# Graph network on one core: 28 products of zeros per unit between an edge layer's product and its transpose

## The chip, the core and the metric

The kernel runs on one core of a Trainium2 chip. The engines are TensorE (PE, with its weight loads shown as PEld), VectorE (DVE), ScalarE (ACT), GpSimd (POOL) and SyncE (SP, which only issues transfers here). The metric is the device time of one execution in microseconds, the median over runs.

## The reference

A residual chain of four graph blocks over 3125 nodes with 128 features and 100000 edges, sorted by destination. The third block matters here. It runs the same edge layer three times:

```python
h = x @ W_enc + b_enc
ea = edge_attr @ W_ee + b_ee            # 16 attributes of an edge -> 128 features
for i in range(3):
    m = relu(h[src] + ea) * edge_atten  # one message of 128 features per edge
    aggr = segment_sum(m, dst)          # summed over the edges of each destination
    z = (1.0 + eps[i]) * h + aggr
    ...                                 # two small matrix products per node, then the next h
```

The other blocks are a two-layer attention convolution, a mean aggregation and a graph attention; the change does not touch them.

## The kernel before

The stages run one after another. In the trace, the two attention convolutions take about the first 3.1 ms (their edge stages are `conv_edges`, with L716, L724 and L768 on TensorE), and the three edge layers of the third block (`gine_edges`, called at L1832) follow, each with a node stage (`gine_nodes`) behind it. Layer 0 runs from about 3408 us to 4538 us, layer 1 from 4604 us, layer 2 from 5811 us. A last aggregation over sources (`by_src`, L1758 on TensorE) ends the kernel.

An edge layer lays the edges out as 128 rows (partitions) of 784 each and goes through them in 98 units of 8 edges per partition (`UNITS = J // UNIT`). For unit j:

- GpSimd gathers h[src] with eight indirect transfers (L1376) of 128 rows of 512 bytes into one of six slots (`RING = 6`). Before unit j it waits until the sum of unit j-6 has been taken (`z_done`).
- TensorE transposes the attributes of the unit (`turn(j)`, L1409) into bank 6 or 7 of PSUM; ScalarE copies them to SBUF (L1399) and spreads a 0/1 mask (L1401).
- TensorE multiplies them with the edge weights: two products of 128x512 in float32 (L1422, four matmul records) into two banks of one of three message buffers in PSUM (`DEEP = 3`). The last of them raises `mm_done`. The product of unit j waits for the copy of its attributes (`copied`), and until the running sum of unit j-3 has released the message buffer (`run_done`).
- VectorE adds the gathered rows in PSUM (L1459, the "sum" of a unit below); it waits for the unit's gathers (`edge_in`) and for `mm_done`. Then it carries the last sum over (L1435, for the unit before), applies relu and the weight (L1465) and forms the running sums of the unit before with a scan (L1442, raises `run_done`).
- ScalarE turns the running sums of that unit back (L1393) and SyncE writes them out (L1384, 512 KB).

The order on each engine is written out by hand. On TensorE it is turn(0), turn(1), and then for each j: product j, turn(j+2). On ScalarE it is for each j: copy j, mask j, rows of unit j-2. So the product of unit j stands on TensorE right ahead of the transpose for unit j+2, and after that transpose TensorE has nothing until the copy of unit j+1, which stands on ScalarE behind the rows of unit j-2.

Of the kernel before, what the change touches and what calls it, by code (L numbers as in the profile page):

```python
# [16 lines left out]
BF, F16 = mybir.dt.bfloat16, mybir.dt.float16  # L17
# [4 lines left out]
P = 128  # L22
# [52 lines left out]
def later(eng, sem, value):  # L75

    if not isinstance(value, int) or value > 0:
        eng.wait_ge(sem, value)


def build(nc, a, out):
    ctx = ExitStack()
    with ctx:
        def sb(name, cols, dt=F32, parts=P):
            return ctx.enter_context(nc.sbuf_tensor(name, [parts, cols], dt))
# [16 lines left out]
        wgt = sb("wgt", 512)  # L102
        bias = sb("bias", 512)
        small = sb("small", 1200)

        psum = ctx.enter_context(nc.psum_tensor("psum", [P, 8 * 512], F32))
        bank = [psum[:, i * 512:(i + 1) * 512] for i in range(8)]


        def dma_sems(*names):  # L110

            count[0] += 1
            return [sem(f"{n}_{count[0]}") for n in names]

        count = [0]

        def fresh(ph, *names):

            count[0] += 1
            sems = [nc.alloc_semaphore(f"{n}_{count[0]}") for n in names]  # L120

            def retire():
                for s in sems:
                    nc.gpsimd.sem_clear(s)
                    nc.release_semaphore(s)
            ph.callback(retire)
            return sems
# [93 lines left out]
        with ExitStack() as ph:  # L221
            pool_step, = fresh(ph, "pool_step0")
            with nc.Block() as block:
                @block.gpsimd
                def _(pool):
                    link_ = Chain(pool, pool_step)
                    for m, base, cm, step in ((ident, 0, 1, -1), (shift_in, -1, -1, 1), (shift_back, 1, -1, 1)):
                        link_(nc.gpsimd.memset(m[:, :], 0.0))
                        link_(nc.gpsimd.affine_select(out=m[:, :], in_=m[:, :], compare_op=ALU.not_equal, fill=1.0, base=base, pattern=[[step, P]], channel_multiplier=cm))
                    link_(nc.gpsimd.memset(ones[:, :], 1.0))  # L230
                    link_(nc.gpsimd.affine_select(out=upper[:, :], in_=ones[:, :], compare_op=ALU.is_gt, fill=0.0, base=0, pattern=[[1, P]], channel_multiplier=-1))

                @block.vector
                def _(dve):
                    nc.vector.memset(x[96:P, :], 0.0)
# [747 lines left out]
        def node_math(body, roots):  # L983

            with ExitStack() as ph:
                step, to_act, from_act = fresh(ph, "math_step", "to_act", "from_act")
                asked = []
                with nc.Block() as block:
                    @block.vector
                    def _(dve):  # L990
                        link = Chain(dve, step)

                        def on_act(func):
                            def run(src, dst, **kw):
                                asked.append((func, src, dst, kw))
                                nc.vector.engine_nop().then_inc(to_act, 1)
                                dve.wait_ge(from_act, len(asked))
                            return run
                        body(link, on_act)

                    @block.scalar
                    def _(act):
                        for n, (func, src, dst, kw) in enumerate(roots):
                            act.wait_ge(to_act, n + 1)
                            nc.scalar.activation(dst, src, func, **kw).then_inc(from_act, 1)
                assert [(f, k) for f, _, _, k in asked] == [(f, k) for f, _, _, k in roots]
# [350 lines left out]
        def gine_edges(layer):  # L1357

            with ExitStack() as ph:
# [10 lines left out]
                with nc.Block() as block:  # L1370
                    @block.gpsimd
                    def _(pool):
                        for j in range(UNITS):
                            later(pool, z_done, j - RING + 1)
                            for k in range(UNIT):
                                nc.gpsimd.indirect_dma_start(  # L1376
                                    out=got[j % RING][:, k * D:(k + 1) * D], out_offset=None, in_=h_tab,
                                    in_offset=bass.IndirectOffsetOnAxis(ap=src_nat[:, UNIT * j + k:UNIT * j + k + 1], axis=0)).then_inc(edge_in[j % RING], 16)
# [26 lines left out]
                    @block.tensor  # L1405
                    def _(pe):
                        def turn(j):
                            later(pe, copied, j - 1)
                            nc.tensor.transpose(bank[6 + j % 2][:, 0:P], ea_nat[:, j * P:(j + 1) * P], ident[:, :]).then_inc(tr_done, 1)  # L1409
                        if layer == 0:  # L1410
                            pe.wait_ge(totalled, 1)
                            nc.tensor.matmul(bank[5][:, 0:1], upper[:, :], in_all[:, 0:1], start=True, stop=True).then_inc(in_all_done, 1)
                            pe.wait_ge(ea_in, 16 * 4)
                        turn(0)
                        turn(1)
                        for j in range(UNITS):
                            if layer == 0 and j == 2:
                                pe.wait_ge(counts_read, 1)
                            pe.wait_ge(copied, j + 1)
                            later(pe, run_done, j - DEEP + 1)  # L1420
                            for k in range(2):
                                ins_ = nc.tensor.matmul(bank[2 * (j % DEEP) + k][:, :], ea_T[j % DEEP], w_blocks[:, k * 512:(k + 1) * 512], start=True, stop=True)  # L1422
                            ins_.then_inc(mm_done, 1)
                            if j + 2 < UNITS:
                                turn(j + 2)

# [195 lines left out]
        def by_src(feat, attention, cin):  # L1622
# [3 lines left out]
            with ExitStack() as ph:  # L1626
# [5 lines left out]
                with nc.Block() as block:  # L1632
# [118 lines left out]
                    @block.tensor  # L1751
                    def _(pe):
                        for n in range(NT):
                            pe.wait_ge(own_ready if attention else diff, pieces_to(n) + 1 if attention else n + 1)
                            for lo in range(0, NP, 512):
                                if attention and n >= NT - 2:
                                    pe.wait_ge(own_ready, pieces_to(n) + 1 + [lo < hi for _, hi in PIECES].index(True))
                                ins_ = nc.tensor.matmul(psum[:, lo:min(lo + 512, NP)], feat[:, n * D:(n + 1) * D], counts[n % R][:, lo:min(lo + 512, NP)],  # L1758
                                                        start=n == 0, stop=True, skip_group_check=True)
                            ins_.then_inc(mm_done, 1)  # L1760
                            if attention:
                                continue
                            if n == 4:
                                pe.wait_ge(to_pe, 1)
                                nc.tensor.matmul(bank[7][:, 0:1], shift_in[:, :], vn1_nat[:, J - 1:J], start=True, stop=True).then_inc(from_pe, 1)
                            if n == 8:
                                pe.wait_ge(to_pe, 2)
                                nc.tensor.matmul(bank[7][:, 1:2], shift_back[:, :], same_nat[:, 0:1], start=True, stop=True)
                                nc.tensor.matmul(bank[7][:, 2:3], shift_in[:, :], fs_nat[:, J - 1:J], start=True, stop=True).then_inc(from_pe, 1)
                            if n == 12:  # L1770
                                pe.wait_ge(to_pe, 3)
                                for k in range(2):
                                    ins_ = nc.tensor.matmul(bank[7][:, (k + 1) * P:(k + 2) * P], srows[:, k * P:(k + 1) * P], ident[:, :], start=True, stop=True)
                                ins_.then_inc(from_pe, 1)
# [225 lines left out]
```

## Time and profile before

| what | us |
| --- | --- |
| median of three runs | 7339.02 |
| lowest and highest | 7315.26, 7345.11 |
| the profiled execution | 7387.36 |
| its span | 7385.6 |
| busy in the span: GpSimd, VectorE, TensorE, ScalarE | 4192.4, 4041.8, 3472.8, 1570.5 |

The mean granted TensorE clock of the profiled execution is 0.636 of full speed. Busy shares are means over stages with different limits; the rows further down are taken from the edge layers and, for comparison, from other stages. A row's "idle before" names what the trace takes to have ended the wait; "remote" and "issue" mean that the trace names nothing. The ends of matmul records are modelled.

### The profile page before, as it was taken

The page shows a single profiled execution, that of the slowest core. Times are in us where ns is not written, and L with a number is a line of the kernel's source. Part 1 is how long each engine was busy: PE and PEld are TensorE (multiplying, and loading weights), DVE is VectorE, ACT ScalarE, POOL GpSimd, SP SyncE. Part 2 cuts the span into 40 slices and gives each one's busy share as a digit, 9 for nine tenths or more (in the row PEclk, how much of TensorE's full clock was granted, in tenths as well). Part 3 has the DMA queues.
Part 4 walks back from the last instruction along what each step waited for, and adds up shares of the span by engine and source line. Part 5 has one row for each costly group of instructions (what it writes and reads, how often), then busy time and mean ns, then how long its engine had stood idle before and what let it go on. Part 6 is the DMA issues. An engine that isn't in the chain of part 4 may idle for free. (4 is left out here: it accounts for less than half of the span.)

```text
span 7385.6 us, 52462 instructions
## 1 busy us (share of the span) xinstructions
PE 3472.8 (47%) x13958; PEld 2190.6 (30%) x13961; DVE 4041.8 (55%) x5328; ACT 1570.5 (21%) x3310; POOL 4192.4 (57%) x4238
## 2 busy tenths in 40 slices
PE   5566555664565565585233334323333423333465
PEld 3445444553454454442111111101111111111133
DVE  5556565664565665675444544434545334445488
ACT  1111111111111111102222222222222222222233
POOL 2555556535655565434766764766665576666321
PEclk7566666675666666686565566555556655556677
DMA  3455555535555555464222322322232222233242
GB/s 99 134 154 152 151 153 156 152 90 145 156 155 155 150 159 149 114 243 127 90 87 86 100 87 81 95 81 91 91 96 89 78 90 87 89 93 96 65 180 98
DMA packets 542142, 876.27 MB, mean 119 GB/s; under 512 B 85127, under 2 KB 383600, under 8 KB 533931
## 3 DMA queue, kind: packets, MB, share of 16 engines
q0 software_dynamic: 167776, 479.21, 21.8%
q1 hardware_dynamic: 373698, 392.93, 17.1%
q8 instruction: 132, 2.16, 0.1%
q14 instruction: 146, 1.20, 0.0%
q10 hardware_dynamic: 390, 0.77, 0.0%
HBM read 552.11 MB, written 320.46 MB: 118 GB/s over the span
## 5 line engine op out<-in xcount | busy, mean ns | idle before, releaser
L1376 POOL DMA_INDIRECT big<-h_tab,big x2352 | 2250.1, 957 | 1136.8 <-issue 822.1
L597 POOL DMA_INDIRECT big<-kv_tab,big x1664 | 1630.9, 980 | 1217.5 <-DVE big L807 680.9
L1422 PE MATMUL psum<-big 128*128 128x512 f32 x1176 | 1059.5, 1054 | 2256.7 <-ACT big L1399 1342.9
L1459 DVE TENSOR_TENSOR psum<-psum,big 128x1024 f32<-128x1024 f32 x294 | 554.5, 1886 | 1766.0 <-remote 1227.0
L1422 PEld LDWEIGHTS psum<-big 128*128 128x128 f32 x1176 | 333.4, 313 | 2822.1 <-ACT big L1399 1482.2
L1393 ACT COPY big<-big 128x1024 f32<-128x1024 f32 x294 | 565.9, 1925 | 2519.6 <-DVE big L1442 2182.2
L724 PE MATMUL psum<-big 128*128 128x128 bf16 x1408 | 568.6, 404 | 971.6 <-issue 500.8
L768 PE MATMUL psum<-big 128*128 128x136 f32 x3328 | 792.2, 398 | 185.1 <-DVE big L838 91.5
L678 ACT COPY big<-psum 125x128 f32<-125x128 f32 x1408 | 376.5, 267 | 2074.7 <-PE psum L724 871.7
L768 PEld LDWEIGHTS psum<-big 128*128 128x128 f32 x3328 | 682.2, 287 | 246.6 <-issue 204.4
L802 DVE TENSOR_TENSOR big<-psum,big 128x512 f32<-128x512 f32 x416 | 286.7, 689 | 825.1 <-remote 616.3
L1442 DVE TENSOR_TENSOR_SCAN big<-big,psum 128x1024 f32<-128x1024 bf16 x294 | 669.7, 2278 | 0.1
L716 PE MATMUL psum<-big 128*128 x4992 | 620.8, 278 | 27.5 <-issue 27.4
L724 PEld LDWEIGHTS psum<-big 128*128 128x128 bf16 x1408 | 209.1, 149 | 1117.5 <-issue 1059.7
L716 PEld LDWEIGHTS psum<-big 128*128 128x128 bf16 x4992 | 471.2, 121 | 116.3 <-issue 33.4
L838 DVE SCALAR_TENSOR_TENSOR big<-big,psum 128x136 f32<-128x136 f32 x832 | 293.2, 352 | 160.7 <-remote 96.9
L1465 DVE SCALAR_TENSOR_TENSOR psum<-psum,big 128x1024 f32<-128x1024 f32 x294 | 360.2, 1225 | 0.4
L1164 POOL DMA_INDIRECT big<-snap_tab,small x60 | 154.6, 2577 | 354.7 <-PE psum L1758 217.4
L1401 ACT CAST big<-big 128x1024 bf16<-128x1024 f32 x294 | 305.1, 1038 | 0.0
L807 DVE TENSOR_TENSOR big<-big 128x512 f32<-128x512 f32 x416 | 283.7, 682 | 0.1
L815 DVE TENSOR_TENSOR big<-big,small 128x512 f32<-128x512 f32 x416 | 283.7, 682 | 0.0
L812 DVE TENSOR_REDUCE big<-big 128x32 f32<-128x512 f32 x416 | 282.3, 679 | 0.7
(405 smaller groups left out, 3376.8 us busy)
## 6 DMA issues: line engine op xcount, KB each, us to landing
run_tab<-big SPq DMA_DIRECT2D x294, 512.0 KB
snap_tab<-big SPq DMA_DIRECT2D x176, 448.0 KB
item_tab<-big SPq DMA_DIRECT2D x208, 272.0 KB
big<-loc_tab SPq DMA_DIRECT2D x104, 512.0 KB
big<-h_tab,big POOLq DMA_INDIRECT x2352
big<-kv_tab,big POOLq DMA_INDIRECT x1664
snap_tab<-big SPq DMA_DIRECT2D x176, 52.0 KB
kv_tab<-big SPq DMA_DIRECT2D x12, 512.0 KB, 2.6
```

The source lines that it names most:

```text
L597: nc.gpsimd.indirect_dma_start(out=kv_ring[:, b % SLOTS, k, :], out_offset=None, in_=kv_tab, in_offset=bass.IndirectOffsetOnAxis(ap=src_it ...
L678: nc.scalar.copy(snaps[0:125, n % 16 * P:(n % 16 + 1) * P], bank[7][0:125, 0:P]).then_inc(snapped, 1)
L716: ins_ = nc.tensor.matmul(bank[b % 2][:, k * P:(k + 1) * P], hot_T[b // 4 % 2][:, (b % 4 * 4 + k) * P:(b % 4 * 4 + k + 1) * P], q3[:, j * ...
L724: nc.tensor.matmul(bank[7][:, 0:P], key_hot[n // 8 % 2][:, n % 8::8], lo_hot[n // 8 % 2][:, n % 8::8], start=first_c + n == 0, stop=True, ...
L768: ins_ = nc.tensor.matmul(region(2 * b + i), hot[b % 2][:, k * P:(k + 1) * P], va[b % 2][:, k, :], start=s == 0, stop=s == 1)
L1376: nc.gpsimd.indirect_dma_start(out=got[j % RING][:, k * D:(k + 1) * D], out_offset=None, in_=h_tab, in_offset=bass.IndirectOffsetOnAxis(ap ...
L1393: nc.scalar.copy(rows_out[j % ROWS].rearrange("p (t f) -> p f t", f=D), sums_ft[j % DEEP].rearrange("p (f t) -> p f t", t=UNIT)).then_inc( ...
L1401: nc.scalar.copy(inner_x[j % DEEP].rearrange("p (f t) -> p f t", t=UNIT), inner[:, UNIT * j:UNIT * (j + 1)].unsqueeze(1).to_broadcast([P, ...
L1422: ins_ = nc.tensor.matmul(bank[2 * (j % DEEP) + k][:, :], ea_T[j % DEEP], w_blocks[:, k * 512:(k + 1) * 512], start=True, stop=True)
L1442: nc.vector.tensor_tensor_scan(sums_ft[j % DEEP], inner_x[j % DEEP], msg[j % DEEP], 0.0, ALU.mult, ALU.add).then_inc(run_done, 1)
L1459: nc.vector.tensor_tensor(by_feature(msg[j % DEEP]), by_feature(msg[j % DEEP]), got[j % RING].rearrange("p (t f) -> p f t", f=D), ALU.add) ...
L1465: nc.vector.scalar_tensor_tensor(by_feature(msg[j % DEEP]), by_feature(msg[j % DEEP]), 0.0, weight_nat[:, UNIT * j:UNIT * (j + 1)].unsquee ...
```

## The change

A tile of zeros (128x128, bf16) is added and set at the start on GpSimd. In each unit of each edge layer, 28 matmuls of zeros by zeros, each with 512 columns, are issued on TensorE behind the unit's product and ahead of the transpose for unit j+2. They write the PSUM bank that this transpose then writes. They wait for nothing and raise no semaphore.

```diff
+        zeros = sb("zeros", P, BF)
 ...
+        def keep_warm(out, count):
+            for _ in range(count):
+                nc.tensor.matmul(out.rearrange("p (k n) -> p k n", n=P), zeros[:, :], zeros[:, :].unsqueeze(1).to_broadcast([P, 4, P]), start=True, stop=True)
 ...
+                    link_(nc.gpsimd.memset(zeros[:, :], 0.0))
                     link_(nc.gpsimd.memset(ones[:, :], 1.0))
 ...
                             ins_.then_inc(mm_done, 1)
+                            keep_warm(bank[6 + j % 2][:, :], 28)
                             if j + 2 < UNITS:
                                 turn(j + 2)
```

## Rows read from the trace of the kernel before

**Rows 1.** Windows by engine, edge layer 0: us; busy PE, PEld, DVE, ACT, POOL; clock; DMA
```profile
3408.00:4530.00 1122.00, 368.61 (x491) 132.26 (x490) 542.74 (x395) 287.77 (x292) 749.72 (x784) 0.58 0.29 91
```

**Rows 2.** The sum's line L1459 by layer: count, duration ns, first and last start
```profile
L1459 DVE TENSOR_TENSOR psum<-psum,big x98: 1856/1877/2127, 3420.4 to 4525.1; 128x1024 f32<-128x1024 f32 x98
...
L1459 DVE TENSOR_TENSOR psum<-psum,big x98: 1858/1877/2004, 4615.8 to 5727.7; 128x1024 f32<-128x1024 f32 x98
...
L1459 DVE TENSOR_TENSOR psum<-psum,big x98: 1861/1877/2019, 5822.2 to 6936.3; 128x1024 f32<-128x1024 f32 x98
```

**Rows 3.** The same line from 3408 to 3520 us, and its waits
```profile
L1459 DVE TENSOR_TENSOR psum<-psum,big x10: 1876/1882/1902, 3420.4 to 3510.4; 128x1024 f32<-128x1024 f32 x10
...
  DMA big<-h_tab,big: 52.5, 10
```

**Rows 4.** Timeline, head of layer 0: gathers, the fourth product, the fourth sum
```profile
3410.33 0.95 POOL L1376 DMA_INDIRECT big<-h_tab,big  x1 [0.30 <-issue]
3411.59 0.95 POOL L1376 DMA_INDIRECT big<-h_tab,big  x1 [0.31 <-issue]
...
3437.93 3.78 PE L1422 MATMUL psum<-big 128*128 128x512 f32 x4 [21.78 <-ACT big L1399]
...
3450.45 1.90 DVE L1459 TENSOR_TENSOR psum<-psum,big 128x1024 f32<-128x1024 f32 x1 [3.72 <-DMA big<-h_tab,big]
```

**Rows 5.** The same line from 3560 to 3840 us, and its waits
```profile
L1459 DVE TENSOR_TENSOR psum<-psum,big x20: 1876/1877/1879, 3564.0 to 3830.0; 128x1024 f32<-128x1024 f32 x20
...
  remote: 152.3, 18
```

**Rows 6.** Timeline around 3900 us (start, us, engine, line): TensorE, VectorE, ScalarE
```profile
3895.43 3.78 PE L1422 MATMUL psum<-big 128*128 128x512 f32 x4 [8.65 <-issue]
...
3908.74 3.78 PE L1422 MATMUL psum<-big 128*128 128x512 f32 x4 [9.31 <-ACT big L1399]
3912.31 0.42 PE L1409 MATMUL psum<-ident,big 128*128 128x128 f32 x1
...
3901.09 1.88 DVE L1459 TENSOR_TENSOR psum<-psum,big 128x1024 f32<-128x1024 f32 x1 [7.76 <-remote]
...
3904.36 2.27 DVE L1442 TENSOR_TENSOR_SCAN big<-big,psum 128x1024 f32<-128x1024 bf16 x1
3915.09 1.88 DVE L1459 TENSOR_TENSOR psum<-psum,big 128x1024 f32<-128x1024 f32 x1 [8.46 <-remote]
...
3906.66 1.92 ACT L1393 COPY big<-big 128x1024 f32<-128x1024 f32 x1 [10.35 <-issue]
3908.39 0.30 ACT L1399 COPY big<-psum 128x128 f32<-128x128 f32 x1
```

**Rows 7.** Counts of sums, products and gathers, layer 0, to 3915.2 (gathers: 3875.3) us
```profile
L1459 DVE TENSOR_TENSOR psum<-psum,big x42: 1871/1877/1999, 3420.4 to 3915.1; 128x1024 f32<-128x1024 f32 x42
...
L1422 PE MATMUL psum<-big x172: 592/1061/1222, 3408.7 to 3911.5; 128*128 128x512 f32 x172
...
L1376 POOL DMA_INDIRECT big<-h_tab,big x336: 939/945/1797, 3408.7 to 3874.2; - x168
```

**Rows 8.** Timeline, conv_edges: TensorE and its reader on ScalarE, dense stretch, then sparse
```profile
730.15 0.40 PE L724 MATMUL psum<-big 128*128 128x128 bf16 x1
...
730.59 0.27 ACT L678 COPY big<-psum 125x128 f32<-125x128 f32 x1 [0.58 <-PE psum L724]
...
739.04 0.41 PE L724 MATMUL psum<-big 128*128 128x128 bf16 x1 [1.51 <-ACT big L678]
739.27 0.89 PE L768 MATMUL psum<-big 128*128 128x136 f32 x4
744.04 0.40 PE L724 MATMUL psum<-big 128*128 128x128 bf16 x1 [3.88 <-ACT big L678]
...
743.63 0.27 ACT L678 COPY big<-psum 125x128 f32<-125x128 f32 x1 [4.74 <-remote]
```

**Rows 9.** Windows of these two stretches, and of the last aggregation
```profile
728.00:736.00 8.00, 7.79 (x45) 6.75 (x46) 6.14 (x12) 1.71 (x8) 3.94 (x5) 0.50 0.44 123
738.90:744.20 5.30, 1.28 (x6) 0.97 (x6) 4.17 (x7) 0.27 (x1) 3.98 (x5) 0.56 0.53 152
...
7070.00:7334.00 264.00, 178.64 (x352) 78.03 (x353) 258.96 (x94) 73.49 (x29) 71.04 (x23) 0.82 0.40 148
```

**Rows 10.** Timeline of the last aggregation: TensorE falls idle, its reader on GpSimd
```profile
7162.85 7.33 PE L1758 MATMUL psum<-big,skip 128*128 128x512 f32 x14 [3.26 <-DVE big L1731]
...
7170.45 3.74 POOL L1164 DMA_INDIRECT big<-snap_tab,small  x1 [6.85 <-PE psum L1758]
```

**Rows 11.** Bf16 products of setup: L524 by stretch, and the windows that hold the clock
```profile
L524 PE MATMUL psum<-big x34: 326/379/379, 91.4 to 97.9; 128*128 128x512 bf16 x23, 128*128 128x384 bf16 x11
...
L524 PE MATMUL psum<-big x10: 527/634/634, 83.4 to 86.9; 128*128 128x512 bf16 x7, 128*128 128x384 bf16 x3
...
92.00:98.00 6.00, 6.00 (x32) 2.99 (x31) 0.00 (x0) 0.00 (x0) 0.00 (x0) 1.00 0.01 3
84.00:87.00 3.00, 3.00 (x10) 1.16 (x8) 2.77 (x11) 0.00 (x0) 0.00 (x0) 0.50 0.00 0
```

**Rows 12.** Timeline, TensorE at the head of layer 0
```profile
3412.33 1.88 PE L1422 MATMUL psum<-big 128*128 128x512 f32 x4
...
3414.16 1.88 PE L1422 MATMUL psum<-big 128*128 128x512 f32 x4
```

**Rows 13.** Timeline, VectorE's sums in a quick stretch, and the end of layer 0
```profile
3855.06 1.90 DVE L1459 TENSOR_TENSOR psum<-psum,big 128x1024 f32<-128x1024 f32 x1 [0.57 <-PE psum L1422]
...
3866.50 1.89 DVE L1459 TENSOR_TENSOR psum<-psum,big 128x1024 f32<-128x1024 f32 x1 [0.42 <-issue]
...
4538.57 0.45 PE L1558 MATMUL psum<-ident,big 128*128 128x128 f32 x1 [13.65 <-PEq L1370]
```

## The prediction

> **What bounds the kernel now.** Four views were read, from the coarse to the fine. The windows by engine say first that no engine is full in an edge layer: of 1122 us TensorE is busy 369, VectorE 543 and GpSimd 750, and the DMA engines 29% [rows 1]. So the layer is paced by waits, and the question is which wait ends last in a unit.
>
> The line view of the sum (L1459, one per unit) shows two paces. The first ten sums of layer 0 start 10.0 us apart ((3510.4 - 3420.4) / 9), and VectorE's wait is for the gathers [rows 3]. Eight gathers at GpSimd's 1.25 us from start to start are 10.0 us [rows 4], so here the gathers pace the layer. Later, from 3564 to 3830 us, 20 sums start 14.0 us apart, and the trace names nobody for the wait ("remote") [rows 5]. Over a whole layer the mean is 11.4 us: (4525.1 - 3420.4) / 97 = 11.39, then 11.46 and 11.49 [rows 2], because short quick stretches at some 5.7 us lie between [rows 13].
>
> The timeline tells what the unnamed wait is. The sum that starts at 3915.09 is the 42nd of its layer; by then 172 matmul records, 43 products, have started, and the 42nd unit's gathers (up to the 336th) were issued by 3875.2 us [rows 7]. At the head of the layer the first sum starts 1.7 us after its eighth gather (3408.7 + 8 x 1.25 = 3418.7 against 3420.4) [rows 3, 4, 7], so by 3915.09 these gathers had landed for some 38 us. The other thing that the sum waits for is the signal of its own product, the 42nd: recorded at 3895.43 and over by 3899.2 [rows 6]. That signal is 15.9 us late against the record, and it comes 6.35 us after the start of the next product, at 3908.74. That next product in turn waits for ScalarE's rows (3906.66) and copy (3908.39), and these for the scan behind the sum before [rows 6]. This closes a loop of 14.0 us: 6.35 from the next product's start to the signal, 7.65 from the sum over VectorE and ScalarE to the product after.
>
> Why the signal is late the trace doesn't name; when it is, it shows. In the convolution's edge stage a bf16 product that ends at 730.55 is read by ScalarE at 730.59, while TensorE is busy 7.79 of 8.00 us around it. One that ends at 739.45 is read at 743.63: TensorE has 0.89 us of work behind it and then nothing until 744.04 [rows 8, 9]. I read this as: a product's result comes on time when TensorE has work behind it, and late when TensorE falls idle, at least while gathers run. Against a general rule stands the last aggregation, where TensorE also falls idle, at 7170.18, and GpSimd goes on at 7170.45 [rows 10]; there GpSimd works 71 of 264 us, against 750 of 1122 here [rows 1, 9]. An edge unit is the sparse case: one product, one short transpose, then idle for 9 us [rows 6].
>
> **The change, part by part.**
> *The setup* gains one small memset on GpSimd, under 1 us, once.
>
> *The 28 products* cost TensorE time. Their price has near relatives in setup: 34 bf16 products with a mean of 471 columns start within 6.5 us at the full 2.4 GHz, 0.197 each, so 0.214 for 512 columns; ten with a mean of 474 within 3.5 us at 1.2 GHz, 0.389 each, so 0.420 [rows 11]. So 28 cost 6.0 us at 2.4 GHz and 11.8 us at 1.2 GHz. The unit's own product and transpose take 1.83 us at 2.4 GHz (3412.33 to 3414.16) [rows 12] and 4.0 us at 1.2 GHz (3908.74 to 3912.73) [rows 6]. A unit is then 7.8 us of TensorE at the high level and 15.8 us at the low one. Under a gather pace of 10.0 us this fits if no more than (10.0 - 7.8) / (15.8 - 7.8) = 27% of the unit's work is done at the low clock, and it breaks even with today's 11.45 us at 46%. Which level will it be? Edge layers are granted 0.58 now with TensorE busy a third of the time; the last aggregation is granted 0.82 with TensorE busy 68%; the stretch in setup that is busy throughout is granted 1.00 [rows 1, 9, 11]. With the zeros TensorE would be busy 78% of a 10 us unit even at the high level, and more at the low one, which lies above the 68%; I take mostly the high level and no loss.
>
> *What stands behind the zeros* on TensorE is the transpose for unit j+2 and then the product j+1; nothing else of TensorE is moved. The transpose is used a whole unit later, so 6 to 12 us cost it nothing at a pace of 10 us. In the gather-paced stretch a product starts as soon as ScalarE has copied, 12.5 us ahead of its own sum (3437.93, 3450.45) [rows 4], and needs 1.7 to 3.8 us, so even a signal 8 us late would still be hidden. VectorE needs 5.5 us a unit (542.74 / 98) and ScalarE 2.9 (287.77 / 98) [rows 1], both hidden under 10.0; without the gathers a unit would cost the 5.7 us of the quick stretches [rows 13].
>
> *The signal's lateness* is what can be won. With 6 us of work right behind each product, the unit looks to TensorE like the dense stretch, where the reader starts 0.04 us after the record's end. The signal then no longer waits for the next product, the 14.0 us loop opens, and the gathers are late next: 10.0 us a unit, for which GpSimd has to run without a pause. The transpose is now the one that is followed by idle time; its lateness falls into its spare unit.
>
> *At a layer's end* 28 products stand behind the last unit's product. They end 6 to 12 us after it, and TensorE is idle there for 13.65 us before the node stage begins [rows 13]: nothing.
>
> **The sum**, against the profiled execution. The sums of the three layers span 1104.7, 1111.9 and 1114.1 us now [rows 2], 3330.7 in all. At 97 x 10.0 = 970 us each they span 2910. That is 420.7 us less: 7387.4 - 421 = 6967 us. The profiled execution lies 0.66% above the median of the runs shown; on the median's scale that is 7339 x 6967 / 7387.4 = 6921, and with a little left for the first units I say 6925 us. Nothing below 10.0 us a unit is in sight, as GpSimd sets it; the lowest run shown (7315) gives 6890 as the low end.
>
> **The rivals.**
> *TensorE becomes the bound (slower).* If the clock stays at 1.2 GHz under the zeros (because zeros don't raise it, or because the idle rest of each unit lowers it again), a unit is 15.8 us: 97 x 15.8 = 1533 us, 3 x 1533 - 3331 = 1267 us more, some 8600 us. It decides from 46% of the work at the low level upwards; between that and all of it lie 7339 to 8600. For it speaks that the clock in edge layers is low in the very stretches where a product runs; against it that continuous work was granted 1.00 [rows 11] after some microseconds at 0.50. A worse form: if the late signals come from results that leave TensorE slowly while gathers run, the zeros queue in the same line. The stretch busy 7.79 of 8.00 us with punctual results [rows 9] speaks against that. Together 0.22.
>
> *The signal stays one product late (no change).* Zeros raise no signal, and if only the next real product brings the late one out, the loop remains 6.35 + 7.65 us; a product of 1.7 instead of 3.6 us might take 1.9 from it in the slow stretches, but the zeros also stand ahead of that next product. About 7340 us. Chance 0.08, the case that the sum waits for something other than TensorE's timing included.
> The Trainium skill's page "SBUF — State Buffer", section "Who interferes with whom", says that TensorE and ScalarE never wait on another engine and that DMA doesn't contend with compute. By that rule the gathers can't make TensorE's results late, the sum waits for something else, and giving TensorE more work would win nothing. The trace doesn't agree: it has late results where gathers are dense and none where they are few [rows 6 to 10], so the rows decide here.
>
> *It works in part.* Some stretches stay at 14 us, or the clock drops now and then: 7000 to 7300 us, chance 0.18.
>
> **How the numbers follow.** The full effect, 6890 to 7000 us, has 0.52; in part 0.18; no change 0.08; slower 0.22, of which a few hundredths lie below 7450. The likeliest is 6925 us, and its own range 6890 to 7000. To leave out no more than 2 in 10 the range runs from 6890 to 7450: 0.52 + 0.18 + 0.08 and some 0.03 of the slower case. About 0.5% (37 us) is what a measurement of this kernel can tell from no change. Faster by more 0.70, within 0.08, slower by more 0.22.
>
> **What would show it.** In the profile after: L1459's starts 10.0 us apart throughout a layer with the gathers as releaser, and no 14.0; GpSimd's gathers every 1.25 us without pause; a granted clock near 0.9 in edge layers; zeros at 0.21 us each. If the zeros are 0.42 us apart and TensorE is busy all the time, the clock rival holds. If L1459 still starts 6 us behind the next product, the signal rival does. The sum is wrong by its size if the gathers slow down once they run without pause, since then 10.0 us isn't their pace over a whole layer.

## The result, and the profile after

The changed kernel takes 7599.15 us (median of three runs, 7597.67 to 7607.19), against 7339.02 before: 1.0376 times as long, with a 95% interval of 1.0352 to 1.0400. The prediction was 6925 us with a range up to 7450, so both its direction and its range were wrong.

The loss is made in the edge layers. These are the sums of the three layers (one window each: line, count, duration in ns, first and last start), to be held against [rows 2]; L1459 has become L1466, since seven lines were added ahead of it.

```profile
L1466 DVE TENSOR_TENSOR psum<-psum,big x98: 1884/1912/2171, 3372.0 to 4570.7; 128x1024 f32<-128x1024 f32 x98
...
L1466 DVE TENSOR_TENSOR psum<-psum,big x98: 1883/1912/2369, 4658.8 to 5859.0; 128x1024 f32<-128x1024 f32 x98
...
L1466 DVE TENSOR_TENSOR psum<-psum,big x98: 1880/1916/2181, 5950.1 to 7148.2; 128x1024 f32<-128x1024 f32 x98
```

They span 1198.7, 1200.2 and 1198.1 us, 3597 in all where it was 3331: 266 us more, 12.36 us a unit instead of 11.45. (The profiled span grew by only 220 us, because the stages ahead, which the change doesn't touch, ended 48 us earlier: first sum at 3372.0 instead of 3420.4.)

The window of layer 0 (the columns as in [rows 1]: TensorE, its weight loads, VectorE, ScalarE, GpSimd, then clock, DMA share, GB/s):

```profile
3360.00:4584.00 1224.00, 929.46 (x3233) 366.94 (x3232) 549.57 (x397) 303.35 (x294) 741.87 (x784) 0.83 0.27 84
```

The clock did what was hoped, 0.83 instead of 0.58. But TensorE is idle for a quarter of a layer that should have been paced by gathers, and GpSimd, meant to work without a pause, is busy 742 of 1224 us. The timeline tells why. First TensorE alone, around the third unit (start, us, engine, line, what, count, idle time before it):

```profile
3377.72 0.27 PE L1415 MATMUL psum<-ident,big 128*128 128x128 f32 x1
3377.82 1.88 PE L1428 MATMUL psum<-big 128*128 128x512 f32 x4
...
3379.76 2.97 PE L113 MATMUL psum<-zeros 128*128 128x512 bf16 x13
3383.69 0.38 PE L113 MATMUL psum<-zeros 128*128 128x512 bf16 x1 [0.96 <-issue]
...
3396.98 0.59 PE L113 MATMUL psum<-zeros 128*128 128x512 bf16 x1 [2.21 <-issue]
3399.78 0.58 PE L113 MATMUL psum<-zeros 128*128 128x512 bf16 x1 [2.21 <-issue]
```

The thirteen zeros of that row start 0.216 us apart ((2.97 - 0.38) / 12), the full-speed price. Then TensorE stalls: one zero per 2.80 us, and "issue" says that the profile knows no wait. A zero is a weight load and a matmul; with all engines shown, the next rows have both:

```profile
3412.38 0.10 PEld L113 LDWEIGHTS psum<-zeros 128*128 128x128 bf16 x1 [2.69 <-issue]
3413.78 0.58 PE L113 MATMUL psum<-zeros 128*128 128x512 bf16 x1 [2.22 <-issue]
...
3415.18 0.10 PEld L113 LDWEIGHTS psum<-zeros 128*128 128x128 bf16 x1 [2.70 <-issue]
3415.20 0.27 ACT L1405 COPY big<-psum 128x128 f32<-128x128 f32 x1 [25.82 <-remote]
...
3415.73 0.95 POOL L1382 DMA_INDIRECT big<-h_tab,big  x1 [0.30 <-issue]
3416.99 0.95 POOL L1382 DMA_INDIRECT big<-h_tab,big  x1 [0.31 <-issue]
...
3426.47 1.88 DVE L1466 TENSOR_TENSOR psum<-psum,big 128x1024 f32<-128x1024 f32 x1 [39.05 <-remote]
...
3461.63 1.91 DVE L1466 TENSOR_TENSOR psum<-psum,big 128x1024 f32<-128x1024 f32 x1 [29.61 <-remote]
```

Load, matmul, load: 3412.38, 3413.78, 3415.18, one instruction of TensorE in 1.40 us, while the gathers go on every 1.25 us. And ScalarE's copy at 3415.20 reads the transpose recorded at 3377.72, 37.5 us before. In between, TensorE has 63 loads and matmuls on record; of the 294 such pairs of a transpose and its copy in the kernel, 290 have a count of 63 or less, and the largest is 66. So a TensorE row is not the moment at which its result can be read: up to some 63 instructions stand between the two, and in this state they move up by one in 1.4 us. Whether the work itself or only its signal comes late, the rows don't tell. (The Trainium skill's page "TensorE: Matmul & The Clock Gate", section "Architectural detail: the array is 16× 32×32, not 1× 128×128", gives TensorE a queue 64 deep; the count agrees.)

It ends when GpSimd stops, waiting for free slots (first GpSimd, then TensorE):

```profile
3449.50 0.94 POOL L1382 DMA_INDIRECT big<-h_tab,big  x1 [0.30 <-issue]
3463.81 0.94 POOL L1382 DMA_INDIRECT big<-h_tab,big  x1 [13.36 <-DVE psum L1466]
...
3455.78 0.58 PE L113 MATMUL psum<-zeros 128*128 128x512 bf16 x1 [2.22 <-issue]
3457.18 2.01 PE L113 MATMUL psum<-zeros 128*128 128x512 bf16 x3 [0.82 <-issue]
3459.98 3.29 PE L113 MATMUL psum<-zeros 128*128 128x512 bf16 x6 [0.79 <-issue]
```

Some 8 us after the last gather the steps shorten to 1.4 and 0.7 us, and from 12 us on TensorE runs without such steps, through the gathers that follow, for some 80 matmuls, until it is held again. This cycle repeats to the end of the layer, but milder: the later steps are mostly 1.4 to 2.8 us, and the pauses of GpSimd shorter.

Most of the loss is made in the first, hard hold. The fourth sum of a layer (at 3461.63 in layer 0) starts 89.6, 89.9 and 88.8 us after the first one, where it was 30.0, 30.2 and 30.1: 178 of the 266 us. Over the other 94 units of a layer the zeros cost 0.3 us a unit.

### The profile page after: what moved, and what is told of

Read it like the earlier page. It is cut to its first block and busy times, and to the rows that moved or that the text cites. A ratio compares the mean times of both kernels' runs of the same rounds, so it can differ in the third digit from the quotient of the medians.

```text
span 7605.4 us, 68930 instructions
## 1 busy us (share of the span) xinstructions
PE 5123.2 (67%) x22193; PEld 2877.8 (38%) x22193; DVE 4051.3 (53%) x5328; ACT 1608.4 (21%) x3310; POOL 4156.3 (55%) x4239
## 5 line engine op out<-in xcount | busy, mean ns | idle before, releaser
L1382 POOL DMA_INDIRECT big<-h_tab,big x2352 | 2224.9, 946 | 1401.3 <-issue 804.2
L113 PE MATMUL psum<-zeros 128*128 128x512 bf16 x8232 | 2187.6, 410 | 770.5 <-issue 751.3
L113 PEld LDWEIGHTS psum<-zeros 128*128 128x128 bf16 x8232 | 831.0, 102 | 2182.7 <-issue 1452.5
L1466 DVE TENSOR_TENSOR psum<-psum,big 128x1024 f32<-128x1024 f32 x294 | 569.8, 1938 | 2020.1 <-remote 1854.7
L1399 ACT COPY big<-big 128x1024 f32<-128x1024 f32 x294 | 582.7, 1982 | 1443.7 <-DVE big L1449 1051.4
L774 PEld LDWEIGHTS psum<-big 128*128 128x128 f32 x3328 | 674.8, 284 | 246.8 <-issue 205.1
L1428 PE MATMUL psum<-big 128*128 128x512 f32 x1176 | 629.6, 651 | 84.5 <-issue 80.5
L1405 ACT COPY big<-psum 128x128 f32<-128x128 f32 x294 | 86.9, 296 | 1317.2 <-remote 1263.7
L1428 PEld LDWEIGHTS psum<-big 128*128 128x128 f32 x1176 | 223.2, 209 | 297.8 <-issue 277.0
```

What stands on the lines that cost most here:

```text
L113: nc.tensor.matmul(out.rearrange("p (k n) -> p k n", n=P), zeros[:, :], zeros[:, :].unsqueeze(1).to_broadcast([P, 4, P]), start=True, stop ...
L774: ins_ = nc.tensor.matmul(region(2 * b + i), hot[b % 2][:, k * P:(k + 1) * P], va[b % 2][:, k, :], start=s == 0, stop=s == 1)
L1382: nc.gpsimd.indirect_dma_start(out=got[j % RING][:, k * D:(k + 1) * D], out_offset=None, in_=h_tab, in_offset=bass.IndirectOffsetOnAxis(ap ...
L1399: nc.scalar.copy(rows_out[j % ROWS].rearrange("p (t f) -> p f t", f=D), sums_ft[j % DEEP].rearrange("p (f t) -> p f t", t=UNIT)).then_inc( ...
L1466: nc.vector.tensor_tensor(by_feature(msg[j % DEEP]), by_feature(msg[j % DEEP]), got[j % RING].rearrange("p (t f) -> p f t", f=D), ALU.add) ...
```

## The experiments

Two theories were left by these rows. **The line:** while gathers run, something that several engines share fills up, and from then on an instruction of TensorE gets through in 1.4 us; zeros are simply more instructions in that line. **The zeros or TensorE:** the columns streamed, the signals or the clock make the delay. Each ratio below is against runs of the kernel before on the same chip. Their medians lay from 7332 to 7404 us, so the ratios are to be compared and not the times. (The times in the expected texts are on the scale of 7339 or of one chip; where a measured time falls outside an expected one for that reason alone, the ratio decides.)

**Size against number.** Zeros of 128 columns instead of 512, still 28:

```diff
-nc.tensor.matmul(out.rearrange("p (k n) -> p k n", n=P), zeros[:, :], zeros[:, :].unsqueeze(1).to_broadcast([P, 4, P]), start=True, stop=True)
+nc.tensor.matmul(out[:, 0:P], zeros[:, :], zeros[:, :], start=True, stop=True)
```

> The change with 28 zero products of 128 columns instead of 512 (a quarter of the columns, as many instructions). In the profile after, TensorE runs some 79 matmuls at full pace and then, while gathers go on, one zero product (a weight load and a matmul) per 2.8 us. Theory 'count': TensorE's instructions leave it at a limited rate while gathers run, whatever their size: as slow as the change, 7550 to 7650 us, with the 2.8 us steps again. Theory 'columns': what counts is the columns streamed: a quarter of the change's loss, 7339 + 260/4 = some 7405 us.

Measured: 7659.98 us, ratio 1.0345 (1.0324 to 1.0365). On the scale of 7339 that is 7592: a quarter of the columns costs as much as all of them. In the held state narrow zeros too stand 2.80 us apart:

```profile
3454.86 0.27 PE L113 MATMUL psum<-zeros 128*128 128x128 bf16 x1 [2.53 <-issue]
3457.66 0.27 PE L113 MATMUL psum<-zeros 128*128 128x128 bf16 x1 [2.53 <-issue]
```

Columns are out; the number of instructions counts. **Fewer zeros,** 7 of 512 columns:

```diff
-keep_warm(bank[6 + j % 2][:, :], 28)
+keep_warm(bank[6 + j % 2][:, :], 7)
```

> The change with 7 zero products of 512 columns instead of 28 (a quarter of the columns and of the instructions). Theory 'count' and theory 'columns' both: about a quarter of the loss, some 7405 us (7370 to 7450). It gives the second point for the price of one zero product. If the zeros helped at all (the prediction's step that work behind a product brings its signal out), a few of them would already make it faster than 7339.

Measured: 7460.21 us, ratio 1.0075 (1.0055 to 1.0095): a fifth of the loss, and no gain. The held units show the step again. A unit has 12 pairs here, 24 instructions, and 24 x 1.4 = 33.6 us is what lies between these two sums, the longest step of each layer:

```profile
3492.91 1.88 DVE L1466 TENSOR_TENSOR psum<-psum,big 128x1024 f32<-128x1024 f32 x1 [23.04 <-remote]
3526.51 1.88 DVE L1466 TENSOR_TENSOR psum<-psum,big 128x1024 f32<-128x1024 f32 x1 [28.05 <-remote]
```

These are TensorE's instructions alone: the three of ScalarE and four of VectorE in such a unit add nothing to the 33.6. By the same account the kernel before, with 5 pairs a unit, has 10 x 1.4 = 14.0 us: its slow pace [rows 5]. **Fewer instructions than before** is the sharper test: no zeros, the unit's product in bf16, two matmuls in place of four passes.

```diff
-w_blocks, w_loaded = area(38600, 8 * D), area(39624, 8 * D)
+w_blocks, w_loaded = area(38600, 4 * D).bitcast(BF), area(39624, 8 * D)
-ea_T = [ring[:, 2 * UNIT * D + k * P:2 * UNIT * D + (k + 1) * P] for k in range(DEEP)]
+ea_T = [ring[:, 2 * UNIT * D + k * P:2 * UNIT * D + k * P + P // 2].bitcast(BF) for k in range(DEEP)]
```

> The kernel before, no zeros, with the unit's product in bf16 (its two operands rounded to bf16): two matmuls where the trace showed four passes, so 3 weight-load and matmul pairs a unit with the transpose, not 5. Theory 'count' with its 2.8 us a pair: 5 x 2.8 = 14.0 us is the slow loop of before, 3 x 2.8 = 8.4 us lies under the gathers' 10.0, so the layers run at the gathers' pace, 97 x 10.0 x 3 = 2910 in place of 3331: some 6925 us. The loop of the prediction (signal 6.35 us after the next product's start, 7.65 us from the sum to the product after): product and transpose shorter by some 2 us in the slow stretches: 7200 to 7300. Theory 'shared' (gathers use up a server that everything shares, at the linear price of the 28 zeros, 0.91 us per 28 pairs): 2 pairs less are worth 294 x 0.065 = 19 us: 7320.

Measured: 7305.62 us, ratio 0.9864 (0.9837 to 0.9891), faster than both kernels, by a small 1.4% against the one before, with an interval clear of 1. The units of 14.0 us are gone, and so are the quick ones. But only the first 20 sums come 10.0 us apart; later ones come 10.8 apart at (3789.2 - 3584.1) / 19, rising to 11.2, and the gathers themselves now take 700.3 / 500 = 1.40 us from start to start:

```profile
L1459 DVE TENSOR_TENSOR psum<-psum,big x20: 1876/1877/1879, 3443.6 to 3633.3; 128x1024 f32<-128x1024 f32 x20
...
L1459 DVE TENSOR_TENSOR psum<-psum,big x20: 1876/1877/1879, 3584.1 to 3789.2; 128x1024 f32<-128x1024 f32 x20
...
  DMA big<-h_tab,big: 97.5, 18
...
L1376 POOL DMA_INDIRECT big<-h_tab,big x501: 940/949/1793, 3699.5 to 4399.8; - x167
```

The 14.0 fell as 'count' has it, but the gain is a quarter of what it said. The time lies in the range of the prediction's loop (7200 to 7300 on 7339, ratios 0.981 to 0.995) by luck: its wait is not to be seen, and the sums now wait for gathers by name. The 10.0 us of [rows 3], on which the prediction and 'count' both rested, is no pace that lasts: after some 160 gathers one takes 1.4 us, with little left for TensorE to do. The bound of a unit is then 8 x 1.4 = 11.2 us.

**Is it TensorE's own line?** 28 one-column copies a unit on ScalarE, none on TensorE:

```diff
+idle_out = area(41600, 14 * UNITS).bitcast(BF)
 ...
+for k in range(28):
+    nc.scalar.copy(idle_out[:, 28 * j + k:28 * j + k + 1], ones[:, 0:1])
 later(act, run_done, j - DEEP + 1)
 nc.scalar.copy(inner_x[j % DEEP]...
```

> The kernel before, no zeros on TensorE, with 28 copies of one column (128 x 1) per unit on ScalarE between its copy of the turned attributes and the spread of the inner flags. Theory 'TensorE alone' (the slow line is TensorE's own): ScalarE works 2.9 of 11.4 us a unit, the small copies fit: 7339, at most some 100 us more where ScalarE's order delays a product. Theory 'shared' (every engine's instructions, or the records of them, use up what the gathers also use): the same price as 28 zeros, some 7600, with TensorE's signals later than before.

Measured: 7993.87 us, ratio 1.0795 (1.0774 to 1.0817), worse than either theory said. ScalarE is held in the same steps, mostly 1.40 us from copy to copy, and runs them 0.093 us apart when the line is empty, some 15 us after the last gather (at 3533.2); 2.15 us hold 22 of them:

```profile
3542.99 0.19 ACT L1402 CAST big<-ones 128x1 bf16<-128x1 f32 x1 [1.21 <-issue]
3544.39 0.19 ACT L1402 CAST big<-ones 128x1 bf16<-128x1 f32 x1 [1.21 <-issue]
3545.09 1.04 ACT L1404 CAST big<-big 128x1024 bf16<-128x1024 f32 x1 [0.51 <-issue]
...
3549.29 2.15 ACT L1402 CAST big<-ones 128x1 bf16<-128x1 f32 x22 [0.41 <-issue]
```

So the hold is not TensorE's alone, and it counts ScalarE's instructions in the same way. A unit has 31 of them here (28 and its own three), and 31 x 1.40 = 43.4 us is what lies between these two sums:

```profile
3476.23 1.88 DVE L1462 TENSOR_TENSOR psum<-psum,big 128x1024 f32<-128x1024 f32 x1 [14.83 <-issue]
...
3519.63 1.88 DVE L1462 TENSOR_TENSOR psum<-psum,big 128x1024 f32<-128x1024 f32 x1 [37.85 <-issue]
```

Each engine thus gets its own instruction through in 1.4 us; those of the other are not added. The rows also speak against two other causes, a full DMA and a late fetch of the program. These are all the DMA queues that moved anything from 3476 to 3520 us, with packets, MB and share:

```profile
q0 software_dynamic: 1129, 2.33, 19.1%
q1 hardware_dynamic: 144, 0.52, 3.0%
```

They were busy a fifth of the time, and the queues that bring instructions (q8 and q14 on the page of the profile) moved no packet, while ScalarE ran 31 instructions one by one. That 28 instructions on ScalarE cost more than 56 on TensorE is not explained by a run of its own; the copies stand in the unit's own chain, ahead of the inner flags and of the rows.

**Who fills it?** The change with half of its gathers:

```diff
-for k in range(UNIT):
+for k in range(UNIT // 2):
     nc.gpsimd.indirect_dma_start(...).then_inc(edge_in[j % RING], 16)
 ...
-dve.wait_ge(edge_in[j % RING], 16 * UNIT * (of_slot(j % RING) + j // RING + 1))
+dve.wait_ge(edge_in[j % RING], 8 * UNIT * (of_slot(j % RING) + j // RING + 1))
```

> The change (28 zero products of 512 columns) with four of a unit's eight gathers left out, so that half of the rows of a unit are old data. Theory 'line' (instructions are held up only while gathers use up what all share): with half the gathers the line has room, no product is held, and TensorE sets the pace with 28 x 0.216 + 1.8 = 7.9 us a unit, every unit the same: 3 x 97 x (12.36 - 7.9) = 1300 us less than the change, some 6380 us on this chip. Theory 'zeros' (the zeros themselves, or the clock, hold TensorE up, whatever gathers do): held steps of 1.4 and 2.8 us stay, and a unit takes over 10 us: above 7000.

Measured: 6345.99 us, ratio 0.8657 (0.8625 to 0.8688). And **eight instructions of GpSimd that are no gathers:**

```diff
-nc.gpsimd.indirect_dma_start(out=got[j % RING][:, k * D:(k + 1) * D], ...).then_inc(edge_in[j % RING], 16)
+nc.gpsimd.memset(got[j % RING][:, k * D:(k + 1) * D], 0.0).then_inc(edge_in[j % RING], 16)
```

> The change (28 zero products of 512 columns) with each of a unit's eight gathers replaced by a memset of the same 128 x 128 tile on GpSimd, as many instructions, no DMA (so no rows are fetched). Theory 'gathers': only an indirect gather takes 1.4 us of what the engines share; then no product is held and TensorE sets 7.9 us a unit throughout, without the tens of us lost at the head of a layer: some 6300 us. Theory 'any instruction': eight instructions of GpSimd a unit fill the line like eight gathers: held steps of 1.4 and 2.8 us on TensorE, a unit over 10 us, above 7000.

Measured: 6321.35 us, ratio 0.8562 (0.8531 to 0.8592). The sums of the two (half of the gathers first) with what they wait for, and a window of the second:

```profile
L1466 DVE TENSOR_TENSOR psum<-psum,big x79: 1916/1919/1925, 3478.3 to 4092.3; 128x1024 f32<-128x1024 f32 x79
...
  PE psum L1428: 166.7, 73
```

```profile
L1464 DVE TENSOR_TENSOR psum<-psum,big x79: 1924/1928/1933, 3481.3 to 4095.3; 128x1024 f32<-128x1024 f32 x79
...
  PE psum L1426: 179.6, 79
...
3340.00:4100.00 760.00, 740.78 (x3058) 348.25 (x3057) 538.36 (x460) 275.35 (x329) 126.27 (x748) 0.98 0.21 74
```

Both run at 614.0 / 78 = 7.87 us a unit, which is TensorE's own time (28 x 0.216 + 1.8), and "remote" has become a plain wait for the product. TensorE does the same 28 zeros a unit on time when the gathers are few or none. With half the gathers one unit of some 33 us stays at the head of each layer, where the first 32 gathers run on without a pause; with memsets the longest step of a whole kernel between two sums of a layer is 8.2 us. Gathers fill the line, other instructions of GpSimd don't, and the number of gathers in a time decides.

**What of a gather counts?** Three runs. A semaphore raised by each of the 28 narrow zeros; on the bf16 product, an eighth of the rows written out in layers 1 and 2; and on the bf16 product, gathers of 64 rows.

```diff
-nc.tensor.matmul(out[:, 0:P], zeros[:, :], zeros[:, :], start=True, stop=True)
+nc.tensor.matmul(out[:, 0:P], zeros[:, :], zeros[:, :], start=True, stop=True).then_inc(mark, 1)
 ...
```

> 28 zero products of 128 columns (7660 us on this chip without this edit), and each of them now raises a semaphore that nobody waits for. Theory 'instructions': the line counts instructions, a signal more on each changes nothing: 7620 to 7700. Theory 'signals': a semaphore's update passes through the same line as an item of its own: half as many items more, some 0.4 to 0.9 us a unit, 7780 to 7930.

```diff
-sp.dma_start(run_rows[:, UNIT * j * D:UNIT * (j + 1) * D], rows_out[j % ROWS])
+sp.dma_start(run_rows[0:16 if layer else P, UNIT * j * D:UNIT * (j + 1) * D], rows_out[j % ROWS][0:16 if layer else P, :])
```

> The bf16 product without zeros (7305 us), with the writing of a unit's rows cut to 16 of 128 partitions in layers 1 and 2, layer 0 whole as a control (so the sums of layers 1 and 2 are wrong). There the gathers themselves are stretched: ten units at 10.0 us, later 11.2 = 8 x 1.4. Theory 'all DMA' (what the gathers use up is shared with the other DMA packets or bytes): an eighth of the writes leaves room, layers 1 and 2 run at 10.0 us a unit, 2 x 97 x 0.96 = 186 us less, some 7120. Theory 'gathers alone': 11.2 us stays in all three layers, 7305.

```diff
-out=got[j % RING][:, k * D:(k + 1) * D], ... ap=src_nat[:, UNIT * j + k:UNIT * j + k + 1]
+out=got[j % RING][0:64, k * D:(k + 1) * D], ... ap=src_nat[0:64, UNIT * j + k:UNIT * j + k + 1]
```

> The bf16 product without zeros (7305 us), with each of the eight gathers of a unit fetching 64 rows instead of 128 (the other half of the rows is old data). Theory 'rows': what a gather uses up goes by its rows, the line has room, and the pace is that of GpSimd at 8 starts: 10.0 us or less a unit, under 7030. Theory 'gathers counted' (each gather instruction is 1.4 us of the line): 11.2 us a unit stays, 7305.

Measured: 7579.78 us, ratio 1.0340 (1.0310 to 1.0370), as without the signals (1.0345; the 7660 us that the expected text names were of another chip); 7235.5 us, ratio 0.9870 (0.9833 to 0.9908), as with all writes; 7217.34 us, ratio 0.9845 (0.9785 to 0.9906), as with all rows. The gathers of the last two, thin writes in layer 1 and half the rows in layer 0:

```profile
L1376 POOL DMA_INDIRECT big<-h_tab,big x430: 940/952/1794, 4899.7 to 5499.7; - x144
```

```profile
L1376 POOL DMA_INDIRECT big<-h_tab,big x501: 893/978/1793, 3700.1 to 4399.5; - x167
```

600.0 / 429 and 699.4 / 500 are 1.40 us again, the first with 53 GB/s of DMA traffic in layer 1 against 95 with all writes. For the gathers' own pace neither the rows nor the traffic beside them count: a gather instruction is 1.4 us with 64 rows as with 128. How TensorE with many zeros fares beside such smaller gathers was not run.

**The threshold.** If the gathers take 8 x 1.4 = 11.2 us a unit and TensorE gets one instruction through in 1.4, then up to 8 of TensorE's instructions are free and 10 are not. One and two zeros of 128 columns behind the bf16 product make just these numbers:

```diff
+keep_warm(bank[6 + j % 2][:, :], 1)
```

> The bf16 product (3 weight-load and matmul pairs a unit with the transpose) plus 1 zero product of 128 columns behind it: 4 pairs. Theory 'one in 1.4': in the filled state a gather takes 1.4 us, and TensorE gets one instruction through in 1.4 us. Then 4 pairs = 8 instructions x 1.4 = 11.2 us, just the gathers' own 8 x 1.4: no loss against the bf16 product alone, ratio to the kernel before 0.985 to 0.992, units at 11.2 us, no run of 14.0. Theory 'smooth price' (each pair costs 0.03 us a unit, whatever its number): 10 us more than the bf16 product alone, ratio 0.988.

```diff
+keep_warm(bank[6 + j % 2][:, :], 2)
```

> The bf16 product plus 2 zero products of 128 columns: 5 pairs a unit, as many as in the kernel before, with a product and zeros that take TensorE 1.1 us a unit instead of 4. Theory 'one in 1.4': 10 instructions x 1.4 = 14.0 us, over the gathers' 11.2: the runs of units at 14.0 us come back, with the quick ones at 5.5 between, and the time is that of the kernel before: ratio 0.996 to 1.004. Theory 'smooth price': 20 us more than the bf16 product alone, ratio 0.989, no 14.0. The prediction's loop (a signal brought out by the next product's start, 6.35 + 7.65 us): with a zero right behind each product no 14.0.

Measured: with one zero 7268.45 us, ratio 0.9849 (0.9819 to 0.9879), no loss; with two 7390.05 us, ratio 1.0007 (0.9993 to 1.0021), the kernel before to within a thousandth. The sums, one zero first:

```profile
L1466 DVE TENSOR_TENSOR psum<-psum,big x21: 1876/1878/1879, 3580.7 to 3798.5; 128x1024 f32<-128x1024 f32 x21
...
  DMA big<-h_tab,big: 101.7, 19
```

```profile
L1466 DVE TENSOR_TENSOR psum<-psum,big x15: 1877/1877/1877, 3591.6 to 3787.6; 128x1024 f32<-128x1024 f32 x15
...
  remote: 109.9, 13
```

With one zero 217.8 / 20 = 10.9 us, and the gathers are named; with two 196.0 / 14 = 14.0 us, and nobody is named. A tiny zero of 128 columns brings the whole slow loop back, and only by its being the ninth and tenth instruction (its load and its matmul).

## Why the prediction was wrong, point by point

- **The two paces and the unnamed wait** [rows 3, 5, 6] were read rightly: gathers landed long before, the sum waited for its product. That the signal is late against the record holds too.
- **The loop of 14.0 us** was the first wrong step. 6.35 + 7.65 us added up, but they were two parts of an interval that is already 14.0 long, and any cut of it adds up. The period is 10 instructions x 1.4 us. The prediction had no second case for its loop; the experiments gave 24 x 1.4 = 33.6, and 14.0 again with a shorter product and a zero right behind it.
- **"A product's result comes on time when TensorE has work behind it"** is the step that failed, and with it the sign. With 28 zeros right behind each product, the sum at 3426.47 still waited 39.05 us; the work behind a product was more to let through, at 1.40 us an instruction, and not what brought its result out. In the convolution the direction of cause seems to be the reverse: TensorE was busy in the dense stretch because nothing held it. GpSimd's gathers say so, five of them in the dense window and five in the sparse one [rows 9]:

```profile
727.22 0.95 POOL L597 DMA_INDIRECT big<-kv_tab,big  x1 [0.30 <-issue]
...
735.23 0.96 POOL L597 DMA_INDIRECT big<-kv_tab,big  x1 [0.30 <-issue]
...
739.00 0.94 POOL L597 DMA_INDIRECT big<-kv_tab,big  x1 [0.30 <-issue]
...
744.19 0.95 POOL L597 DMA_INDIRECT big<-kv_tab,big  x1 [0.30 <-issue]
```

  They start (735.23 - 727.22) / 4 = 2.00 us apart in the dense stretch and (744.19 - 739.00) / 4 = 1.30 in the sparse one: over and under the 1.4 that the runs found. That this explains the convolution too is argued from these rows; no run changed that stage.
- **The rival's worse form,** "results leave TensorE slowly while gathers run, the zeros queue in the same line", is what happened. It had no time and no chance of its own, only a part in the 0.22 of the slower case, on the strength of that same dense stretch.
- **The price of the zeros** was right, 0.214 forecast and 0.216 measured, and the clock rose as forecast (0.83, "near 0.9"). So the clock rival fell, too: with the gathers gone the same zeros ran at 0.98 and 7.87 us a unit, against 7.8 forecast.
- **The floor of 10.0 us a unit** was mis-sized. It came from ten units at the head of a layer [rows 3, 4]; after some 20 units it is 11.2, and over a whole layer of the bf16 product (below) 1062.9 / 97 = 10.96. The signals on time were then worth what the bf16 product won, about 1.4%, and not 5.6%. The prediction named this risk in its last sentence and gave it no chance of its own.

```profile
L1459 DVE TENSOR_TENSOR psum<-psum,big x98: 1876/1877/1881, 3443.6 to 4506.5; 128x1024 f32<-128x1024 f32 x98
```

- **Where the 266 us come from:** two thirds are the first hold at the head of each layer, where sums stand up to 56 us apart. After it a unit's 33 pairs pass the held line at 1.4 to 2.8 us each, and the long steps between sums are 12 to 25 us; GpSimd runs out of free slots and stops; the line empties; TensorE then runs some 80 matmuls unheld. In the middle of layer 0 GpSimd's gathers make 8 x 700.1 / 464 = 12.07 us a unit, where it was 8 x 699.9 / 485 = 11.54 (the kernel before first). Between pauses they start 1.25 us apart in both kernels; the pauses differ, in which GpSimd waits for a sum to free a slot: 24 of 3.9 us before, 23 of 5.3 us after.

```profile
L1376 POOL DMA_INDIRECT big<-h_tab,big x486: 939/945/1797, 3700.0 to 4399.9; - x162
...
  DVE psum L1459: 94.4, 24
```

```profile
L1382 POOL DMA_INDIRECT big<-h_tab,big x465: 942/947/957, 3699.9 to 4400.0; - x155
...
  DVE psum L1466: 122.8, 23
```

Of the Trainium skill's page "SBUF — State Buffer", section "Who interferes with whom", the prediction said that the trace disagrees. The runs bear that out in numbers: instructions of TensorE and ScalarE 1.40 us apart while gathers run, and zeros 0.216 and copies 0.093 us apart when not held. The section is about access to SBUF; no run here shows that this access is what is held.

**What stays open** is what the line is. It counts instructions of TensorE and ScalarE, at least, beside GpSimd's gathers: on TensorE not columns or semaphores, of the gathers not rows. The Trainium skill's page "NOTIFIC — the notification-queue block", section "7.1 Overflow: three behaviours, one of which stalls the engine", says that the block which writes out an engine's records holds producers back inside rather than lose a record. That would fit, but every run here was recorded, so no run tells whether the line is there without the recording. Why it takes about 20 units of gathers, or some 80 matmuls beside them, to fill was not tried either.

## What to carry to other kernels

When an engine waits for nobody, list the starts of several engines and look for a common step: in these runs 1.4 us on TensorE, ScalarE and GpSimd said "one line" where any single wait suggested a loop. Where GpSimd issues gathers densely, count the instructions of TensorE and ScalarE, not their length: up to 8 of TensorE a unit were free, the ninth and tenth brought the units of 14.0 us back, and dropping some (two bf16 matmuls for four fp32 passes: 1.4% won) was worth more here than keeping an engine busy. And test a correlation in a trace with the smallest dose first, one zero rather than 28, since "busy, hence punctual" can as well be "not held, hence busy".

## What the runs showed that I had not expected

- A gather costs 1.40 us in the long run of the bf16 product, though GpSimd starts one in 1.25 us for some 160 gathers; 64 rows cost as much as 128.
- An engine's small instructions can be held to one in 1.4 us by another engine's gathers, with "issue" as the only name for it, and in the two stretches shown it took 12 and 15 us after the last gather until they ran freely.
- A TensorE row can stand 37.5 us, and 63 instructions, ahead of the moment at which its result can be read.
- 28 zeros a unit raise the granted clock from 0.58 to 0.83, and that is worth nothing here.
